# Attention stage of a four-stage kernel: from a barrier at each step to waits for producers, with a pair's work laid in five steps

## The chip, the cores and the metric

The program runs on one core of one Trainium2 chip. The time is device microseconds of one execution, from 3 runs of the kernel before. The core has four engines that compute, each with its own instruction queue that runs strictly in order: PE (TensorE), DVE (VectorE), ACT (ScalarE) and POOL (GpSimd); SP issues most transfers. Engines wait for one another by semaphores.

## The reference, cut to what matters

The model has four stages. Only the first, L0_attn, is touched. It takes x of 32 sequences x 256 tokens x 128 features:

```python
xn = _layernorm(x, ln1_g, ln1_b)
q = _l2norm((xn @ Wq).reshape(Bx, Tx, H, Dh))     # 16 heads of 8
k = _l2norm((xn @ Wk).reshape(Bx, Tx, H, Dh))
v = (xn @ Wv).reshape(Bx, Tx, H, Dh)
clock = softplus(xn @ clock_w + clock_b)
q, k = _rope(q, times), _rope(k, times)
gcp = exp(clip(cumsum(-softplus(xn @ gate_w + gate_b), axis=1), -60., 50.))
q, k = q * gcp, k / (gcp + 1e-08)
p = xn @ p_w + p_b
p_exp = exp(p - max(p, axis=1)) * clock
q = q / (cumsum(p_exp, axis=1) + 1e-08)
k = k * p_exp
attn = softmax(where(mask, einsum('bqhd,bkhd->bhqk', q, k) / sqrt(Dh), -inf))
x1 = einsum('bhqk,bkhd->bqhd', attn, v).reshape(Bx, Tx, D) @ out_w + out_b + x
h = _layernorm(x1, ln2_g, ln2_b)
return x1 + gelu(h @ mlp_w1 + mlp_b1) @ mlp_w2 + mlp_b2
```

The second stage norms each token, picks one of 8 experts by the largest affinity and applies it; the kernel computes affinity and place of a token at the end of attention and scatters its row there. Then come a state-space layer (the scan stage) and a coupling network with gelus.

## The kernel before

The function attention() works on pairs of sequences: 16 pairs (PAIRS) of 512 tokens (STEP), held as 4 tiles (TS) of 128 tokens, or turned, as 128 features x 512 tokens. Each engine runs a function of its own (pe_step, act_step, dve_step, pool_step, sp_step) once per step k, in an order written out by hand. In step k four things run side by side:

- the front of pair k: layer norm (bn statistics, a root as Ln and Exp on ACT, xn), the transposes into xt, projections for gate, clock, p, q, k, their swapped forms for the rotation, and v, each into bank FA or FB by turns; softplus as Abs, Exp, Ln; the running sums; q_t, the masked copies k_m (L723) and v_a (L711). POOL makes xl, the residual with the first norm, which goes to HBM and comes back as xlb_m.
- the scores of pair k-1: eight quads. quad(n) (L431) writes four scores blocks into the four RING banks, exps(n) (L606) takes them through Exp to es, weigh(n) (L450) multiplies them with v_a into the one bank AV. After two quads ACT copies AV out (av_copy), PE turns it back (back, L467), and DVE divides by the sums (heads_out, L733).
- the tail of pair k-2: o_tok turned, times out_w, x1, its norm h_tok, MLP (four times up, gelu, all through the one bank M, then down, L543), x2, its norm y_n, y1 (row), its norm xl2, the affinities (L586). mv_m, rs_m, stats_m, h_tok, o_t and M are single.
- the route of pair k-3: the best expert, its rank by a small matmul into AV (L488), the position, and four indirect DMAs from POOL (L921).

q_t, k_m, v_a, x_in, row and o_tok exist twice; xt, rot, mag, log, pre, factor, lnorm, square and pexp once. Gelu needs another table of ACT than Exp and Ln: a table is loaded at L664 and back at L665, and at the head of each step (L594).

At the end of a step each engine drains and raises end_pe, end_act, end_dve or end_pool, and begin() (L372) lets none start the next step before all four have. The steps are k = 0 to 18: four written out, a loop Fori with two steps in its body (k = 4 to 15), three written out. SP loads x_in one pair ahead, and xlb_m and x_m, once DVE and POOL have ended the step before.

## Time and profile before

| what | us |
|---|---|
| median of 3 runs (lowest, highest) | 2848.79 (2848.25, 2849.33) |
| the profiled execution's own time | 2853.14 |
| its span | 2851.4 |
| PE / DVE / ACT / POOL busy over the span | 2018.1 / 1834.8 / 1576.2 / 1162.6 |
| mean granted TensorE clock | 0.867 |

The page shows one profiled execution. Its slices of 71 us show the attention stage as the first fifteen: PE at 6 to 7 tenths, ACT at 5 to 6, DVE at 5. A timeline row gives start, duration, engine, line, operation, written and read tile and their shape; xN means that N instructions were merged; in brackets stands how long the engine idled ahead of it and what ended that. "<-issue" is a wait for nothing that the profile shows, "ACTq" the queue of an engine at its drain. The granted clock is 1.0 at 2.4 GHz and 0.5 at 1.2 GHz. L594 runs at the start of a step on ACT and so marks the steps: 42.6, 84.3, 134.2, 193.1 (k = 3), then every 60 to 62 us to 988.4 (k = 16), 1031.6 and 1068.3.

### The profile page before, as it was taken

Reading aid. Unit: us, or ns where it says so; the run is one execution under the profiler, and the core shown is the slowest. Engines: PE = TensorE matmul, PEld = TensorE weight load, DVE = VectorE, ACT = ScalarE, POOL = GpSimd, SP = SyncE. Lnnn points to the kernel's source line nnn. Section 1 sums busy time; section 2 is a strip of 40 time slices with the busy share of each in tenths; the row PEclk is TensorE's granted clock in tenths of the full one; section 3 lists DMA queues with packets and bytes.
Section 4 is the critical chain, followed back from the end, with each engine's and each line's share of the span. In section 5 each row is a group of like instructions: output and inputs, shape, how many; then the busy total and the mean of one; then the engine's idle time right before and its main releaser. Section 6 shows DMA issues by size and latency. Waiting matters only on the chain. (4 is left out here: it accounts for less than half of the span.)

```text
span 2851.4 us, 39979 instructions
## 1 busy us (share of the span) xinstructions
PE 2018.1 (71%) x11854; PEld 1037.9 (36%) x11909; DVE 1834.8 (64%) x3731; ACT 1576.2 (55%) x2903; POOL 1162.6 (41%) x718
## 2 busy tenths in 40 slices
PE   2677777777777763666646787777777777658886
PEld 0344444444444443556522222222222222124432
DVE  5565665555565522222225999999999999946665
ACT  1566666566666642444436666666666666435443
POOL 1111211211221112344325888888888878710000
PEclk7799998889899886888878899989999998878887
DMA  3000000000000001111111111112121111011111
GB/s 121 23 16 20 23 21 27 27 20 20 21 22 20 24 16 33 37 45 41 37 49 47 48 49 41 41 44 56 47 55 40 40 41 49 22 34 30 45 37 45
DMA packets 137060, 105.16 MB, mean 37 GB/s; under 512 B 12872, under 2 KB 130776, under 8 KB 136544
## 3 DMA queue, kind: packets, MB, share of 16 engines
q1 hardware_dynamic: 131424, 89.48, 11.3%
q0 software_dynamic: 5504, 13.90, 1.4%
q8 instruction: 85, 1.39, 0.2%
q14 instruction: 47, 0.39, 0.0%
HBM read 42.18 MB, written 27.59 MB: 24 GB/s over the span
## 5 line engine op out<-in xcount | busy, mean ns | idle before, releaser
L1738 POOL TENSOR_TENSOR hc<-h,c_rep 128x1024 f32<-128x1024 f32 x256 | 602.4, 2369 | 157.4 <-DVE h L1696 150.0
L1696 DVE TENSOR_TENSOR_SCAN h<-decay,bank 128x1024 f32<-128x1024 f32 x256 | 572.6, 2268 | 0.0
L1582 ACT ACTIVATE decay<-bank,neg_a_r 128x510 f32<-128x510 f32 x512 | 322.4, 682 | 323.4 <-PE bank L1473 275.8
L1687 DVE TENSOR_TENSOR bank<-bank,b_rep 128x1024 f32<-128x1024 f32 x256 | 304.3, 1216 | 53.7 <-PE bank L1460 53.0
L1460 PE MATMUL bank<-u,sel_u 128*128 128x512 bf16 x489 | 166.1, 421 | 234.9 <-DVE h L1696 227.9
L613 ACT ACTIVATE es<-bank 128x384 f32<-128x384 f32 x512 | 208.5, 493 | 52.9 <-PE bank L447 52.6
L1460 PEld LDWEIGHTS bank<-u,sel_u 128*128 128x128 bf16 x512 | 33.6, 99 | 408.5 <-DVE h L1696 363.7
L1473 PE MATMUL bank<-d,sel_u 128*128 128x512 bf16 x481 | 168.8, 424 | 6.4 <-ACT decay L1582 2.2
L901 POOL TENSOR_TENSOR xl<-x_in,f_mean_var 128x512 f32<-128x512 f32 x16 | 17.0, 1062 | 363.3 <-ACT f_rstd L604 363.3
L914 POOL TENSOR_TENSOR mag<-mag,one_up 128x512 f32<-128x512 f32 x16 | 20.5, 1282 | 338.7 <-ACT one_up L675 338.7
L1487 PE MATMUL bank<-hc,y_sel 128*32 128x512 f32 x1024 | 146.7, 647 | 4.6 <-POOL hc L1738 4.6
L424 PE MATMUL bank<-xt,w_a 128*128 128x512 f32 x224 | 135.8, 709 | 17.5 <-DVE pre L806 9.1
L1281 DVE SCALAR_TENSOR_TENSOR o<-bank,xs,xls 128x128 f32<-128x128 f32 x72 | 25.1, 349 | 177.6 <-PE bank L1148 89.2
L1234 ACT ACTIVATE hid<-bank 128x512 f32<-128x512 f32 x72 | 43.0, 597 | 169.0 <-PE bank L1136 165.7
L1494 PE MATMUL bank<-xpad,w_conv 128*128 128x512 f32 x256 | 124.4, 620 | 2.9 <-ACT xc L1625 1.4
L1124 PE MATMUL bank<-consts,xns 128*128 128x128 f32 x72 | 25.8, 360 | 138.6 <-ACT xns L1220 118.2
L439 PE MATMUL bank<-q_t,k_m 32*128 32x256 f32 x1024 | 103.3, 476 | 28.5 <-ACT es L613 23.1
L738 DVE RECIPROCAL rec<-bank 128x16 f32<-128x16 f32 x64 | 16.5, 257 | 157.7 <-PE bank L471 157.2
L1183 POOL COPY w_tile<-w 128x512 f32 x72 | 44.2, 614 | 177.1 <-PE bank L1136 160.5
L1903 PE MATMUL bank<-r_o_t,w_c 128*128 128x512 f32 x96 | 73.7, 885 | 41.4 <-DVEq L2114 20.6
L1136 PE MATMUL bank<-xst,w_tile 128*128 128x128 f32 x576 | 100.2, 329 | 0.0
L921 POOL DMA_INDIRECT rows_in_dram<-row,idx x64 | 76.6, 1197 | 52.2 <-DVEq L891 28.0
(333 smaller groups left out, 4727.4 us busy)
## 6 DMA issues: line engine op xcount, KB each, us to landing
xvs<-xv SPq DMA_DIRECT2D x16, 512.0 KB, 3.0
xs<-rows_in_dram SPq DMA_DIRECT2D x72, 68.0 KB
w<-in_w_dram SPq DMA_DIRECT2D x2, 2048.0 KB
x_in<-in_x_dram SPq DMA_DIRECT2D x16, 256.0 KB
xlb_dram<-xl SPq DMA_DIRECT2D x16, 256.0 KB, 2.3
xlb_m<-xlb_dram SPq DMA_DIRECT2D x16, 256.0 KB, 3.8
x_m<-in_x_dram SPq DMA_DIRECT2D x16, 256.0 KB, 3.7
g_xn<-yx_dram SPq DMA_DIRECT2D x16, 256.0 KB
```

The lines of the kernel that those rows point to most:

```text
L424: pe.matmul(bank[:, :], weight, xt[:, :], start=True, stop=True).then_inc(sem, 1)
L439: pe.matmul(RING[st][:, 0:T], kk[:, 0:P], q, start=True, stop=True, tile_position=(32 * st, 0))
L613: last = act.activation(es[(n % 2) * HS + st][:, :], RING[st][:, 0:3 * P], ACT.Exp, scale=DH ** -0.5)
L1136: last = pe.matmul(bank[:, f * P:(f + 1) * P], w1[j][:, f * P:(f + 1) * P], xt[j][:, :], start=False, stop=True, skip_group_check=True)
L1460: last = pe.matmul(BD[n % 2][:, i * STEP:(i + 1) * STEP], c["sel_u"][:, r, :], u3[p if n < NS else q][:, hf, st + i, :], start=True, stop= ...
L1473: pe.matmul(DL[i], c["sel_u"][:, r, :], d3[p if n < NS else q][:, hf, st + i, :], start=True, stop=True).then_inc(s["n_d"], 1)
L1487: last = pe.matmul(Y[32 * st:32 * st + 32, :], c["y_sel"][:, r, :], hc[(2 * i + st // 2) % 4][:, st % 2, :], start=False, stop=r == 3, til ...
L1494: last = pe.matmul(seq(G), c["w_conv"][:, tap, hf * P:(hf + 1) * P], xpad[:, :, tap:tap + T], start=tap == 0, stop=tap == TAPS - 1)
L1582: act.activation(decay[n % 4][:, i, :, 1:], seq(DL[i])[:, :, 1:], ACT.Exp, scale=c["neg_a_r"][:, hf, g:g + 1]).then_inc(s["n_da"], 1)
L1687: dve.tensor_tensor(pair_of(BD[n % 2]), pair_of(BD[n % 2]), b_rep[p if n < NS else q][:, :].unsqueeze(1).to_broadcast([P, 2, STEP]), ALU.m ...
L1696: dve.tensor_tensor_scan(flat(h[n % 4]), decay[n % 4].rearrange("p i b t -> p (i b t)"), BD[n % 2], 0.0, ALU.mult, ALU.add).then_inc(s["n_ ...
L1738: pool.tensor_tensor(hc[n % 4][:, :, :], h[n % 4][:, :, :], c_rep[p][:, :].unsqueeze(1).to_broadcast([P, 2, STEP]), ALU.mult).then_inc(s[" ...
```

## The change

begin(), the four end semaphores and the drains are gone. Every wait now names a producer, or by since(), which leaves out counts that are not positive, the last reader of a tile that is to be written again. The flags of a step are ln, front, scores, late, mid, tail, and a pair runs through five steps: its norm and xt in step k-1, its front in k, quads 0 to 5 and weighs 0 to 4 in k+1, the rest of the scores, heads_out(2) and (3) and x1 with its statistics in k+2 (late, mid), h_tok, MLP, y1, affinities and scatter in k+3 (tail). The steps are k = -1 to 18: six written out, a loop of four rounds with two steps (k = 5 to 12), six written out. There are a second xt and a tile rot_k beside rot; xn and o_tok are turned through M, the ranks go to FA instead of AV. SP loads x_in two pairs ahead. The table load at the head of a step is gone; Abs of mag stands ahead of the fourth gelu.

The written orders of a full step, with u the pair of the scores (k-1), w that of the late part (k-2):

- PE: gate; turn h_tok; clock; up(0); p; up(1); q; up(2); weigh(5,w); up(3); quad(6,w); down; back(2,w); quad(7,w); q swapped; weigh(6,w); weigh(7,w); quad(0,u); turn xn; ones for q; back(3,w); quad(1,u); k; weigh(0,u); turn xl2; weigh(1,u); quad(2,u); k swapped; back(0,u); quad(3,u); affinities; ones for k; weigh(2,u); weigh(3,u); turn o_tok; quad(4,u); ranks; out_w; back(1,u); quad(5,u); v; weigh(4,u).
- ACT: v_a; h_t; gelus 0 to 2; Abs; gelu 3; table; Exp and Ln of mag; exps(6,w); av_copy(2,w); pexp; square q; root ln; exps(7,w); one_up three times; exps(0,u); av_copy(3,w); root of x2; xt; exps(1,u); root of y1; lgcp twice; exps(2,u); av_copy(0,u); o_t; square k; Ln pcs; Ln lnorm; exps(3,u); neg; Exp factor q; o_t; exps(4,u); av_copy(1,u); Ln lnorm; exps(5,u); root of x1; Exp factor k; k_m.
- DVE: h_tok; pre twice; pmax, pneg; statistics of x_in; softplus and sum of the gate; heads_out(2,w); first of q's rotation; x2 and statistics; xn; y_n, y1, statistics; rest of q's rotation; heads_out(3,w); xl2; lnorm q; the clock's softplus, pexp, pcs; first of k's rotation; factor q; heads_out(0,u); affinities and best expert; rest of k's rotation; positions; q_t; lnorm k; factor k; x1 and statistics; heads_out(1,u); rot_k times factor, times pexp.
- POOL: xl in three; mag and log; four scatters; x1b.

The diff, cut to its core:

```diff
@@ attention @@
-        def begin(eng, k):
...
-            for sem in (s["end_pe"], s["end_act"], s["end_dve"], s["end_pool"]):
-                eng.wait_ge(sem, k)
+        def since(eng, sem, count):
...
+            if not isinstance(count, int) or count > 0:
+                eng.wait_ge(sem, count)
...
-        xt = sb("xt", [P, STEP])
+        xt = [sb(f"xt{n}", [P, STEP]) for n in range(2)]
...
+        rot_k = sb("rot_k", [P, STEP])
...
+        def pe_step(pe, k, half, p, ln, front, scores, late, mid, tail):
...
             if front:
+                pe.wait_ge(s["f_xt_sb"], k + 1)
+                since(pe, s["f_mk"], k)
+                project(FB, c["w_gate"], s["f_gate"])
             if tail:
+                pe.wait_ge(s["m_h"], k - 2)
+                transposes(M, h_tok, s["m_ht"])
+            if front:
+                since(pe, s["f_vaug"], k)
+                project(FA, c["w_clock"], s["f_clock"])
             if tail:
+                up(0)
...
+            if late:
+                weigh(5, k - 2, p)
+            if late:
+                quad(6, k - 2, p)
...
+            if late:
+                back(2, k - 2)
+                quad(7, k - 2, p)
+            if front:
+                pe.wait_ge(s["f_pe"], k + 1)
+                project(FB, c["w_qs"], s["f_qs"])
+            if late:
+                weigh(6, k - 2, p)
+            if late:
+                weigh(7, k - 2, p)
+                quad(0, k - 1, q)
+            if ln:
+                pe.wait_ge(s["f_xn"], k + 2)
+                if tail:
+                    pe.wait_ge(s["m_x2"], k - 2)
+                transposes(M, xn, s["f_xt"])
...
+            if late:
+                back(3, k - 2)
+                quad(1, k - 1, q)
+            if front:
+                pe.wait_ge(s["f_rb"], k + 1)
+            if scores:
+                weigh(0, k - 1, q)
...
+            if scores:
+                weigh(1, k - 1, q)
+                quad(2, k - 1, q)
+            if front:
+                pe.wait_ge(s["f_mq"], k + 1)
+                back(0, k - 1)
+                quad(3, k - 1, q)
...
+                weigh(2, k - 1, q)
+            if scores:
+                weigh(3, k - 1, q)
+            if mid:
+                pe.wait_ge(s["s_o"], 8 * k - 8)
+                if tail:
+                    pe.wait_ge(s["m_aff_sb"], k - 2)
+                elif ln:
+                    pe.wait_ge(s["f_xt_sb"], k + 2)
+                transposes(M, o_tok[p], s["m_ot"])
+            if scores:
+                quad(4, k - 1, q)
+            if tail:
+                pe.wait_ge(s["r_hot"], k - 2)
...
-            pe.drain().then_inc(s["end_pe"], 1)
...
+        def act_step(act, k, half, p, ln, front, scores, late, mid, tail):
...
+            if scores:
+                act.wait_ge(s["f_v"], k)
...
+                act.activation(v_a[q][:, :, :, 0:DH], FA.rearrange("p (j h d) -> p j h d", j=TS, h=H), ACT.Copy).then_inc(s["f_vaug"], 1)
+                act.wait_ge(s["m_ht"], k - 2)
...
+                act.activation(h_t[:, :], M[:, :], ACT.Identity, scale=c["ln2_g"], bias=c["ln2_b"]).then_inc(s["m_ht_sb"], 1)
...
+                for n in range(FC):
+                    if n == FC - 1 and front:
+                        act.wait_ge(s["f_pre1"], k + 1)
...
+                        act.activation(mag[:, :, :], pre[:, :, :], ACT.Abs).then_inc(s["f_abs"], 1)
+                    act.wait_ge(s["m_up"], 4 * k + (n - 11))
+                    act.activation(g[:, n, :], M[:, :], ACT.Gelu, bias=c["mlp_b1"][:, n:n + 1]).then_inc(s["m_gelu"], 1)
+                act.preload_act_table_set(EXP_LN)
...
+            if late:
+                exps(6, k - 2)
+                av_copy(2, k - 2)
...
+            if late:
+                exps(7, k - 2)
...
+            if scores:
+                exps(0, k - 1)
+            if late:
+                av_copy(3, k - 2)
+                root(mv_m[:, :, 1], ln_m[:, :], rs_m[:, :], s["m_mv2"], s["m_ln2"], s["m_rs2"], k - 2, bias=EPS)
...
+                exps(1, k - 1)
+            if tail:
+                root(vv_m[:, :, :], vv_m[:, :, :], row[q][:, :, RS0:RS1 + 1].rearrange("p j v -> p v j"), s["m_vv3"], s["m_ln3"], s["m_rs3"], k - 2)
...
+                exps(2, k - 1)
+                av_copy(0, k - 1)
...
+                exps(3, k - 1)
+            if tail:
+                act.wait_ge(s["r_neg"], k - 2)
+                act.activation(neg[:, :], neg[:, :], ACT.Exp).then_inc(s["r_exp"], 1)
...
+                exps(4, k - 1)
+                av_copy(1, k - 1)
+            if front:
+                act.wait_ge(s["f_mk"], k + 1)
+                exps(5, k - 1)
+            if mid:
+                root(mv_m[:, :, 1], ln_m[:, :], rs_m[:, :], s["m_mv"], s["m_ln"], s["m_rs"], k - 1, bias=EPS)
...
+                act.wait_ge(s["f_zk"], k + 1)
+                act.wait_ge(s["f_k2"], k + 1)
...
+                    last = act.activation(k_m[p][:, v, :], rot_k[:, :], ACT.Copy, scale=c["head_mask"][:, v:v + 1])
...
+        def dve_step(dve, k, half, p, ln, front, scores, late, mid, tail):
...
+            if late:
+                heads_out(2, k - 2, p)
+            if front:
+                turned(rot, FA, FB, s["f_ra"], s["f_sq"], s["f_rb"], s["f_qs"], s["f_rq"], 0)
...
+                dve.wait_ge(s["m_dn"], k - 2)
+                dve.tensor_tensor(x2[:, :, :], tok(M), x1b[:, :, :], ALU.add).then_inc(s["m_x2"], 1)
...
+            if ln:
+                dve.wait_ge(s["f_rs"], k + 2)
...
+                centred(xn, x_in[q], mv, rs[:, 1, :], s["f_xn"])
+            if tail:
+                dve.wait_ge(s["m_rs2"], k - 2)
+                centred(h_tok, x2, mv_m, rs_m, s["m_yn"])
...
+                dve.tensor_tensor(row[q][:, :, 0:D], h_tok[:, :, :], x_m[:, :, :], ALU.add).then_inc(s["m_y1"], 1)
...
+                stats_of(dve, row[q][:, :, 0:D], stats_m, mv_m, s["m_st3"], s["m_mv3"], k - 2)
+                two_variances(dve, vv_m, mv_m[:, :, 1], s["m_vv3"])
+            if front:
+                turned(rot, FA, FB, s["f_ra"], s["f_sq"], s["f_rb"], s["f_qs"], s["f_rq"], 1)
+            if late:
+                heads_out(3, k - 2, p)
...
+                                         row[q][:, :, RS0:RS1 + 1], ALU.mult, ALU.mult)
+                centred(xl2, row[q][:, :, 0:D], mv_m, row[q][:, :, RS0], s["m_xl2"])
...
+            if scores:
+                heads_out(0, k - 1, q)
+            if tail:
+                dve.wait_ge(s["m_aff"], k - 2)
+                dve.tensor_copy(aff[:, :, :], M[:, 0:TS * E].rearrange("p (j e) -> p j e", j=TS)).then_inc(s["m_aff_sb"], 1)
...
+                turned(rot_k, FB, FA, s["f_ka"], s["f_sk"], s["f_kb"], s["f_ks"], s["f_rk"], 1)
+                chain(dve.tensor_tensor(pos[:, :, :], FA[:, 0:TS * E].rearrange("p (j e) -> p j e", e=E),
...
+                dve.tensor_tensor(q_t[p][:, :], rot[:, :], factor[:, :], ALU.mult).then_inc(s["f_qt"], 1)
...
+                dve.tensor_scalar(lnorm[:, :], FB[:, :], 1e-24, None, ALU.max).then_inc(s["f_mk"], 1)
...
+                dve.scalar_tensor_tensor(factor[:, :], lnorm[:, :], -0.5, lgcp[:, :], ALU.mult, ALU.subtract).then_inc(s["f_zk"], 1)
...
+                dve.wait_ge(s["m_ow"], k - 1)
...
+                dve.tensor_tensor(x1[:, :, :], tok(M), xlb_m[:, :, :], ALU.add).then_inc(s["m_x1"], 1)
...
+                stats_of(dve, x1, stats_m, mv_m, s["m_st"], s["m_mv"], k - 1)
+                heads_out(1, k - 1, q)
...
+                dve.tensor_tensor(rot_k[:, :], rot_k[:, :], factor[:, :], ALU.mult).then_inc(s["f_k1"], 1)
...
+                dve.tensor_tensor(rot_k[:, :], rot_k[:, :], pexp[:, :], ALU.mult).then_inc(s["f_k2"], 1)
...
+            def one(k, half, p):
+                step(eng, k, half, p, k < PAIRS - 1, 0 <= k < PAIRS, 1 <= k < PAIRS + 1, 2 <= k < PAIRS + 2, 2 <= k < PAIRS + 2, 3 <= k)
...
+            for k in range(-1, 5):
+                one(k, k // 2, k % 2)
+            with eng.Fori(0, (PAIRS - 8) // 2) as n:
+                step(eng, n * 2 + 5, n + 2, 1, True, True, True, True, True, True)
+                step(eng, n * 2 + 6, n + 3, 0, True, True, True, True, True, True)
+            for k in range(PAIRS - 3, PAIRS + 3):
+                one(k, k // 2, k % 2)
```

## Rows read from the trace of the kernel before

**Rows 1.** The table of windows: both stretches, then busy us (x instructions) per engine.

```profile
core 0: us, PE busy (x) PEld busy (x) DVE busy (x) ACT busy (x) POOL busy (x), PEclk, DMA share, GB/s
193.10:988.40 795.30, 604.81 (x5292) 367.61 (x5293) 463.70 (x1470) 503.21 (x1015) 159.01 (x130) 0.90 0.08 23
1000.00:1032.00 32.00, 25.82 (x287) 16.49 (x284) 8.21 (x41) 18.31 (x40) 2.87 (x3) 0.97 0.03 10
```

**Rows 2.** Timeline of PE: start us, us, instruction; the first matmul of two steps.

```profile
621.76 1.09 PE L428 MATMUL bank<-consts,o_tok 128*128 128x128 f32 x4 [4.10 <-issue]
...
681.75 0.66 PE L428 MATMUL bank<-consts,o_tok 128*128 128x128 f32 x2 [1.84 <-ACTq L725]
```

**Rows 3.** Timeline of PE, then ACT, where only scores ran.

```profile
1013.42 0.71 PE L439 MATMUL bank<-q_t,k_m 32*128 32x256 f32 x8
...
1014.83 0.64 PE L459 MATMUL bank<-es,v_a 128*32 128x256 f32 x8
...
1015.29 0.40 PE L463 MATMUL bank<-es,v_a 128*32 128x128 f32 x8
...
1014.61 1.64 ACT L613 ACTIVATE es<-bank 128x384 f32<-128x384 f32 x4 [2.00 <-PE bank L447]
...
1018.99 0.63 ACT L620 ACTIVATE avs<-bank 128x512 f32<-128x512 f32 x1
```

**Rows 4.** Timeline of ACT in one full step.

```profile
632.67 0.21 ACT L602 ACTIVATE m_ln<-m_mean_var 128x4 f32<-128x4 f32 x1 [3.05 <-DVE m_mean_var L387]
...
638.14 1.06 ACT L648 ACTIVATE mag<-mag 128x1024 f32<-128x1024 f32 x1
...
644.95 0.69 ACT L664 ACTIVATE g<-bank,vec 128x512 f32<-128x512 f32 x1 [1.22 <-PE bank L479]
...
649.47 1.28 ACT L665 ACT_TABLE_LOAD   x1
...
679.06 2.55 ACT L723 ACTIVATE k_m<-rot,consts 128x512 f32<-128x512 f32 x4
```

**Rows 5.** Timeline of PE in the same step.

```profile
637.37 0.60 PE L428 MATMUL bank<-consts,h_tok 128*128 128x128 f32 x4
...
644.75 1.02 PE L424 MATMUL bank<-xt,w_a 128*128 128x512 f32 x2
645.69 1.12 PE L479 MATMUL bank<-h_t,w_a 128*128 128x512 f32 x2
```

**Rows 6.** Timeline of DVE, then POOL, in the same step.

```profile
623.86 3.79 DVE L755 TENSOR_SCALAR xn<-x_in,f_mean_var,f_rstd 128x128 f32<-128x128 f32 x4 [1.63 <-ACT f_rstd L604]
630.62 0.69 DVE L784 TENSOR_TENSOR x<-bank,xlb_m 128x512 f32<-128x512 f32 x1 [2.98 <-PE bank L501]
...
634.25 0.18 DVE L793 TENSOR_TENSOR pos<-bank,fill 128x32 f32<-128x32 f32 x1
...
635.63 0.72 DVE L806 TENSOR_SCALAR pre<-bank,vec 128x512 f32<-128x512 f32 x1
...
660.70 1.11 DVE L755 TENSOR_SCALAR h_tok<-x,m_mean_var,m_rstd 128x128 f32<-128x128 f32 x4
...
664.20 0.26 DVE L738 RECIPROCAL rec<-bank 128x16 f32<-128x16 f32 x1
...
623.99 1.11 POOL L901 TENSOR_TENSOR xl<-x_in,f_mean_var 128x512 f32<-128x512 f32 x1 [23.17 <-ACT f_rstd L604]
```

**Rows 7.** Timeline of PE: the same work in two neighbouring steps.

```profile
605.74 2.03 PE L565 MATMUL bank<-square,consts 128*128 128x512 f32 x2 [2.05 <-DVE rot L747]
...
668.41 1.12 PE L565 MATMUL bank<-square,consts 128*128 128x512 f32 x2 [2.05 <-DVE rot L747]
```

**Rows 8.** Timelines of ACT, DVE and POOL at the stage's two ends.

```profile
84.31 1.28 ACT L594 ACT_TABLE_LOAD   x1
...
1038.60 1.11 DVE L755 TENSOR_SCALAR h_tok<-x,m_mean_var,m_rstd 128x128 f32<-128x128 f32 x4 [0.58 <-ACT m_rstd L604]
...
1078.45 0.96 POOL L921 DMA_INDIRECT rows_in_dram<-row,idx  x1 [0.30 <-issue]
```

More of the change, by code:

```diff
@@ L566, in pe_step @@
-            if scores:
-                quad(6)
-                weigh(5)
-            if front:
-                pe.wait_ge(s["f_kb"], rf)
-                for j in range(TS):
-                    last = pe.matmul(FA[:, j * P:(j + 1) * P], xt[:, j * P:(j + 1) * P], c["w_v"], start=True, stop=True)
-                last.then_inc(s["f_v"], 1)
-            if scores:
-                back(2)
-                quad(7)
-                weigh(6)
-            if tail:
-                pe.wait_ge(s["m_xl2"], rm)
-                transposes(M, xl2, s["m_x2t"])
@@ new lines, in pe_step @@
+            if mid:
+                pe.wait_ge(s["m_ot_sb"], k - 1)
+                for j in range(TS):
+                    last = pe.matmul(M[:, j * P:(j + 1) * P], o_t[:, j * P:(j + 1) * P], c["w_o"], start=True, stop=True)
+                last.then_inc(s["m_ow"], 1)
+            if scores:
+                back(1, k - 1)
+                quad(5, k - 1, q)
+            if front:
+                pe.wait_ge(s["f_kb"], k + 1)
+                if tail:
+                    pe.wait_ge(s["r_pos"], k - 2)
+                for j in range(TS):
+                    last = pe.matmul(FA[:, j * P:(j + 1) * P], xt[p][:, j * P:(j + 1) * P], c["w_v"], start=True, stop=True)
+                last.then_inc(s["f_v"], 1)
@@ new lines, in act_step @@
+            if front:
+                if not tail:
+                    act.wait_ge(s["f_pre1"], k + 1)
+                    since(act, s["f_soft"], k)
+                    act.activation(mag[:, :, :], pre[:, :, :], ACT.Abs).then_inc(s["f_abs"], 1)
+                act.wait_ge(s["f_abs"], k + 1)
+                act.activation(mag[:, :, :], mag[:, :, :], ACT.Exp, scale=-1.0).then_inc(s["f_exp"], 1)
+                act.wait_ge(s["f_exp"], k + 1)
+                since(act, s["f_sp"], k)
+                act.activation(log[:, 0, :], mag[:, 0, :], ACT.Ln, bias=1.0).then_inc(s["f_log"], 1)
```

598 lines of the change are left out of this document (245 added, 353 removed).

## The prediction

> **What bounds the kernel now.** I read the page's slices first: the attention stage ends near 1080 us [rows 8], and nothing behind it is touched. Then the table of windows over its thirteen full steps (k = 3 to 15): 795.3 us, 61.2 each, in which TensorE (PE) is busy 46.5, ScalarE (ACT) 38.7, VectorE (DVE) 35.7 and GpSimd (POOL) 12.2 [rows 1]. No engine is full; even PE lacks 24%. So the handing over between engines sets the step, the barrier being one part of it. What the barrier alone costs is seen on PE: it idles 1.84 us ahead of a step's first matmul, and 4.10 where the loop jumps back [rows 2]. That is some 3 us of a step's 14.7 us of PE idleness; the other 12 lie inside the step, where PE waits for ACT's exponentials and copies and for DVE's rotations and norms. Taking the barrier away is worth 3 us at most; the rest depends on whether the new order shortens the way work goes round the engines.
>
> **What sets the new step.** Without a barrier a step's length is the longest closed round of waits: from one instruction to the same one a step later, along each engine's written order and each semaphore. I walked the new order from the listing with the durations of the old one. The prices:
> - a quad takes PE 1.41 us until the next operation (1013.42 to 1014.83), and lets its exponentials start after 1.19; a weigh takes 0.86 (1014.83 to 1015.69); four exponentials 1.62, a copy of AV 0.62 [rows 3];
> - a root 0.45, a table load 1.28, an exponential of 128x1024 1.07, one gelu 0.69, the four k_m copies 2.6, one 128x512 activation 0.6 to 0.65 [rows 4];
> - four transposes 0.53 to 0.6, a projection 0.94 (644.75 to 645.69), an up-projection 1.12, 1.16 until its gelu can start [rows 5];
> - a DVE pass over 128x512 0.7, x1 with its statistics 2.05 (630.62 to 632.67), y_n to the two variances 3.5 (660.70 to 664.20), xl2 1.2, the position chain 1.4 (634.25 to 635.63), one heads_out 0.6 [rows 4, 6].
>
> The longest round that I find closes over 16 legs, from weigh(3) to weigh(3):
> 1. PE: weigh(3), transposes of o_tok, quad(4), ranks: 0.86 + 0.53 + 1.41 + 0.4 = 3.2
> 2. DVE: positions, q_t, lnorm for k: 1.4 + 0.7 + 0.7 = 2.8
> 3. ACT: Ln of lnorm: 0.65
> 4. DVE: factor for k, then x1 and statistics: 0.7 + 2.05 = 2.75
> 5. ACT: root, Exp of factor: 1.1
> 6. DVE: two products into rot_k: 1.4
> 7. ACT: k_m, then v_a: 2.6 + 0.6 = 3.2
> 8. PE: clock projection, into the bank that v_a frees, up(0): 0.94 + 1.16 = 2.1
> 9. gelu and up in turn on the one bank M, each with a projection or weigh(5) between: 2.1 + 2.1 + 2.0 + 0.7 = 6.9
> 10. ACT: table load, Exp and Ln of mag, exps(6), AV copy: 1.28 + 1.07 + 0.55 + 1.6 + 0.6 = 5.1
> 11. PE: back(2), quad(7), q's swapped projection, weigh(6), weigh(7), quad(0): 0.55 + 1.41 + 0.94 + 1.72 + 1.19 = 5.8
> 12. ACT: exps(0), AV copy, root for y_n: 2.7
> 13. DVE: the y_n block, second half of q's rotation, heads_out(3), xl2: 3.5 + 1.4 + 0.6 + 1.2 = 6.7
> 14. PE: transposes, weigh(1), quad(2): 2.6
> 15. ACT: exps(2), AV copy: 2.25
> 16. PE: back(0), quad(3), affinities, ones product, weigh(2) behind heads_out(0): 0.55 + 1.41 + 1.0 + 1.0 + 0.86 + 0.3 = 5.1
>
> The legs sum to 54.4, and some ten hand-overs of 0.05, seen from a gelu's end at 645.64 to PE's start at 645.69 [rows 4, 5], make 55.0. So the order still goes round the engines in series; it is shorter than the old one, not free.
>
> **The clock.** These are prices at TensorE's 2.4 GHz. The granted clock of the full steps was 0.90, so a fifth of the time lay at the 1.2 GHz level; at that level the same product took 2.03 us instead of 1.12 [rows 1, 7]. PE's legs above hold about 25 us, so a share f at the lower level adds 25 x 0.8 x f. Where PE was busy 81% of a stretch the grant was 0.97, f = 0.06 [rows 1]; the new steps would be busy some 44 of 56, 79%. I take f = 0.08: 1.5 us, and a step of 56.5.
>
> **What else moves.** The second xt and the second rotation tile let work start early; they add no instruction. The x_in load is issued two pairs ahead and xlb_m and x_m behind the readers of their tiles; each has tens of us to land, so SP's queue costs nothing, and if a load were late it would stand before DVE's x1 or y1, on the round. POOL's four instructions of scatter keep their length; x1b now stands behind them and is needed only at x2, over 25 us later. The table load at each step's start goes, but it ran while ACT had to wait for PE's first transposes anyway, so nothing is gained. Abs now stands between two gelus. No row shows an Abs under the gelu table; if it forces two loads, they cost 2.56 a step on leg 9, if not zero. I take zero. The Trainium skill (ScalarE: Activation LUTs, Table sets) says that cheap functions such as abs are in every set; no row here shows it. POOL's arithmetic slows DVE: xn took 3.79 for four instructions beside xl, y_n of the same shape 1.11 without [rows 6]. xn runs now in a gap in which DVE would wait for leg 12's root, at no cost; x1b may fall on leg 6 or on h_tok, 0 to 2.5 us, and I take 0. The loop jumps back 3 times instead of 5; PE's jump cost 2.3 us, and PE has some 2.5 us of slack at that place of the new round, so I count 0, between -5 (two jumps fewer) and +7 (three in full) in all.
>
> **Both ends.** Before, step 0 ended at 84.3, and the full steps began at 193.1 [rows 1, 8]. Step 0 must still go once through a pair's front; the norm of pair 1 now lies in it and its 3.79 of xn delays q's rotation: it ends near 87. Step 1 has its norm behind it and only six quads, by the same walk 36; step 2 adds quads 6 and 7 with their copies and x1: 45. So the thirteen full steps begin at 168. Behind them, step 16 is the round without the front's legs 2 to 8 in part, 11 and 13 in part: 42. Step 17 is a lone MLP, in the old trace 32 us from its h_tok at 1038.60 to the end of its affinities, and 5 for the next pair's x1: 37. Step 18 is h_tok to the last scatter, 1038.60 to 1079.4: 41 [rows 8]. A last pair that is spread over more steps thus gives back some 28 us of what the full steps gain.
>
> **The sum.** 168 + 13 x 56.5 + 42 + 37 + 41 = 1022.5, where the last scatter ended at 1079.4 [rows 8]: 56.9 us saved. The profiled execution took 2853.1 (span 2851.4), 4.3 over the median of 2848.8; so 2796.2 in a profile, 2791.9 as a median, say 2792.
>
> **The rivals.**
> - PE becomes the bound, 0.16. If a leg of my round isn't on it (an engine that comes early and lets two legs overlap), the step falls towards PE's own 44 to 46.5. At 47 the end is at 168 + 611 + 120 = 899, 180 earlier: 2668; at 52, between, 2733. For it: PE's 46.5 is all that is unavoidable. Against: ACT, DVE and PE take turns in the round, in written order.
> - The clock stays as it was, 0.14. With f = 0.20 PE's legs rise by 25 x 0.8 x 0.2 = 4.0: 59.0 a step, 2824. For it: drops follow waits of 2 us as short as that ahead of L565, which once ran slow and once fast [rows 7].
> - Slower than before, 0.09. Place: PE's legs. Instead of a long idle stretch at each barrier PE now has many of 1 to 2 us, and if these keep it at 1.2 GHz for half the time, a step costs 55 + 10 = 65, and the total is 2848.8 + 13 x 65 + 288 - 1079.4 = 2902. It decides from 60.9 a step (791.4 / 13), f = 0.30. Against: 0.97 at 81% busy. The Trainium skill (TensorE: Matmul & The Clock Gate, A second HAM failure mode) tells of a kernel whose short idles between matmul groups made the clock swing; by that rule this rival, by the row at 1000 us the forecast.
> - The change doesn't do what it says: a wait for the slowest engine survives, each step near 60.5, within 0.2% of before, 0.03.
>
> **How the numbers follow.** The forecast, 54 to 58.5 a step (2759 to 2818), has 0.58. The range reaches into the faster case to 52.3 a step and into the clock's to 59.5: 2737 to 2830; outside stay most of PE's case and the slower one, some 0.2. A difference of 0.2% (5.7 us) is about what a measurement of this kernel can tell from none. Faster: 0.58 + 0.16 + 0.14 = 0.88; within: 0.03; slower: 0.09.
>
> **What would show it.** Right: full steps of 54 to 58 us; PE idle ahead of the clock projection for v_a, ahead of k's projection for rot_b, and ahead of weigh(2) and weigh(4) for DVE; a granted clock of 0.94 or more in the full steps; the last three steps about 120 us together. Wrong: a step of 50 or less with PE over 90% busy (a leg isn't on the round); a granted clock of 0.90 or less; table loads beside Abs; or a stage end that comes over 130 us after the last k_m.

## The result, and the profile after

The changed kernel took 2828.84 us (median of 4, 2823.87 to 2829.27) beside 2849.06 for the kernel before: a ratio of 0.9918, with a 95% interval from 0.9899 to 0.9937. So 20 us are saved; the prediction had 57. In the two profiled executions it is 24.4 (2853.14 and 2828.72; spans 2851.4 and 2826.9).

All times below come from three marks in each trace: the end of ScalarE's k_m copies of pair 2 (start of the thirteen full steps), the same of pair 15 (their end), and the end of the last scatter (the end of the stage). For the kernel before the marks are those of [rows 1, 8]. Behind the last scatter the span has 1772.8 us after and 1772.0 before: nothing changed there.

| us | before | forecast | after |
|---|---|---|---|
| start | 193.1 | 168 | 172.0 |
| 13 full steps (one) | 795.3 (61.2) | 734.5 (56.5) | 744.2 (57.24) |
| the rest, to the last scatter | 91.0 | 120 | 137.9 |
| stage | 1079.4 | 1022.5 | 1054.1 |

The windows of the changed kernel: the full steps, and then the three steps in which the last pairs run out (us, then busy us and instructions of each engine, the granted clock, DMA share, GB/s).

```profile
core 0: us, PE busy (x) PEld busy (x) DVE busy (x) ACT busy (x) POOL busy (x), PEclk, DMA share, GB/s
172.00:916.00 744.00, 590.11 (x5285) 362.66 (x5285) 482.24 (x1453) 483.09 (x998) 145.19 (x127) 0.90 0.08 23
916.00:972.00 56.00, 39.95 (x376) 24.75 (x377) 15.88 (x73) 24.00 (x54) 5.14 (x5) 0.77 0.05 15
972.00:1013.00 41.00, 25.66 (x170) 15.68 (x169) 13.00 (x67) 12.99 (x26) 3.54 (x4) 0.67 0.04 12
1013.00:1054.00 41.00, 18.57 (x61) 11.10 (x59) 8.94 (x47) 7.73 (x13) 5.40 (x6) 0.54 0.02 7
```

The clock of the full steps is what it was in [rows 1], 0.90. DVE is busy 482 us in them where it had 464 in 51 us more: its instructions became longer (it is 462 once x1b is moved, see below). The last three rows are nearly steps 16, 17 and 18. The clock falls to 0.54 in them, near its 1.2 GHz level throughout.

Where leg 6 of the round lies, DVE and POOL (timelines; start, duration):

```profile
677.73 2.28 DVE L972 TENSOR_TENSOR rot_k<-rot_k,factor 128x512 f32<-128x512 f32 x1 [0.26 <-ACT factor L782]
680.04 0.69 DVE L974 TENSOR_TENSOR rot_k<-rot_k,pexp 128x512 f32<-128x512 f32 x1
...
677.18 0.96 POOL L998 DMA_INDIRECT rows_in_dram<-row,idx  x1 [0.30 <-issue]
678.17 1.28 POOL L1003 TENSOR_TENSOR x1b<-x,rows 128x512 f32<-128x512 f32 x1
```

The first of two products of one shape takes 2.28 us, the second 0.69. The first lies beside POOL's x1b, which runs right behind the scatters until 679.45. It is on the round: k_m waits for it. At the end of step 16 x1b lies beside h_tok instead, which takes 2.84 us there and 1.11 elsewhere (DVE, then POOL):

```profile
968.45 2.84 DVE L819 TENSOR_SCALAR h_tok<-x,m_mean_var,m_rstd 128x128 f32<-128x128 f32 x4 [2.29 <-issue]
...
969.15 1.27 POOL L1003 TENSOR_TENSOR x1b<-x,rows 128x512 f32<-128x512 f32 x1
```

k_m and the jump of the loop:

```profile
623.39 2.56 ACT L786 ACTIVATE k_m<-rot_k,consts 128x512 f32<-128x512 f32 x4 [3.14 <-DVE rot_k L974]
...
620.60 0.43 PE L478 MATMUL bank<-es,v_a 128*32 128x128 f32 x8
624.46 2.07 PE L435 MATMUL bank<-xt,w_a 128*128 128x512 f32 x2 [3.43 <-issue]
...
677.62 1.08 PE L474 MATMUL bank<-es,v_a 128*32 128x256 f32 x8 [2.14 <-DVE o_tok L805]
```

These are ScalarE, then TensorE, at a jump of the loop. PE stands 3.43 us for nothing that the profile shows, where in [rows 2] it was 4.10; then the clock projection runs at 1.2 GHz (2.07; 0.94 to 1.02 in [rows 5]). The last row is the wait for DVE ahead of weigh(4) that the prediction named.

Gelu's table load stands in two ways. First a pass of the loop, then a step that is written out (ScalarE):

```profile
628.30 1.28 ACT L678 ACT_TABLE_LOAD   x1
630.38 0.69 ACT L678 ACTIVATE g<-bank,vec 128x512 f32<-128x512 f32 x1 [0.80 <-PE bank L494]
...
634.78 1.05 ACT L676 ACTIVATE mag<-pre 128x1024 f32<-128x1024 f32 x1
636.10 0.69 ACT L678 ACTIVATE g<-bank,vec 128x512 f32<-128x512 f32 x1 [0.27 <-PE bank L494]
...
744.64 1.28 ACT L678 ACT_TABLE_LOAD   x1 [3.25 <-PE bank L494]
745.94 0.69 ACT L678 ACTIVATE g<-bank,vec 128x512 f32<-128x512 f32 x1
```

In the loop the load runs while up(0) runs. In the written-out steps from k = 4 on it stands behind the wait for up(0), and the whole 1.28 us come on top. What decides the place isn't shown: step 3, written out, waits only for up(0) and has the load early (173.15); step 4 waits for w_down's reader too and has it late (233.26); but the steps of the loop have both waits in the program and the load early. Abs (L676) stands between two gelus, and no load comes with it.

### The profile page after: what moved, and what is told of

The parts are those of the page before. It is cut to its first block and busy times, and to the rows that moved or that the text cites. A ratio compares the mean times of both kernels' runs of the same rounds, so it can differ in the third digit from the quotient of the medians.

```text
span 2826.9 us, 39859 instructions
## 1 busy us (share of the span) xinstructions
PE 2013.0 (71%) x11854; PEld 1035.8 (37%) x11909; DVE 1861.9 (66%) x3731; ACT 1552.1 (55%) x2885; POOL 1154.5 (41%) x718
## 5 line engine op out<-in xcount | busy, mean ns | idle before, releaser
L998 POOL DMA_INDIRECT rows_in_dram<-row,idx x64 | 66.5, 1039 | 434.7 <-DVE row L947 420.0
L435 PE MATMUL bank<-xt,w_a 128*128 128x512 f32 x224 | 152.5, 777 | 39.9 <-ACT v_a L666 20.4
L474 PE MATMUL bank<-es,v_a 128*32 128x256 f32 x1024 | 85.6, 405 | 39.2 <-DVE o_tok L805 35.8
L494 PE MATMUL bank<-h_t,w_a 128*128 128x512 f32 x128 | 90.9, 799 | 15.9 <-ACT g L678 12.6
L1224 PE MATMUL bank<-w,hid 128*128 x576 | 95.4, 317 | 1.1 <-ACT hid L1310 1.1
```

The lines of the kernel that those rows point to most:

```text
L435: pe.matmul(bank[:, :], weight, xt[p][:, :], start=True, stop=True).then_inc(sem, 1)
```

## The experiments

Each kernel is one or more edits of the changed kernel and computes the same. They ran in four groups, each beside the kernel before on its own chip (there 2838.8 to 2840.8), so the totals are compared as ratios and the stages by their marks. The changed kernel itself was run again beside the second group.

| kernel | ratio to before [95%] | start | one full step | rest | stage |
|---|---|---|---|---|---|
| the change | 0.9918 [0.9899, 0.9937] | 172.0 | 57.24 | 137.9 | 1054.1 |
| after_same_chip | 0.9905 [0.9889, 0.9922] | 171.2 | 57.24 | 134.4 | 1049.7 |
| barrier_back | 0.9998 [0.9987, 1.0009] | 175.6 | 58.39 | 148.0 | 1082.6 |
| x1b_later | 0.9792 [0.9773, 0.9810] | 171.4 | 54.89 | 134.1 | 1019.0 |
| xl_later | 0.9883 [0.9864, 0.9902] | 165.6 | 57.01 | 133.7 | 1040.4 |
| gelu_table | 0.9874 [0.9858, 0.9891] | 172.3 | 56.52 | 130.9 | 1038.0 |
| root_early | 0.9904 [0.9887, 0.9920] | 172.3 | 57.12 | 133.2 | 1048.2 |
| all | 0.9763 [0.9747, 0.9779] | 165.9 | 54.55 | 122.4 | 997.5 |
| warm | 0.9863 [0.9846, 0.9879] | 170.7 | 56.83 | 125.6 | 1035.1 |
| unrolled | 0.9952 [0.9934, 0.9971] | 170.7 | 58.02 | 134.4 | 1059.4 |
| gelu_unrolled | 0.9864 [0.9843, 0.9886] | 172.1 | 56.51 | 131.5 | 1038.3 |
| warm_unrolled | 0.9849 [0.9826, 0.9872] | 171.4 | 56.29 | 125.5 | 1028.7 |
| all_unrolled | 0.9749 [0.9730, 0.9767] | 165.3 | 54.60 | 128.6 | 1003.8 |
| all_warm | 0.9741 [0.9717, 0.9765] | 167.5 | 55.04 | 115.7 | 998.7 |
| all_warm_unrolled | 0.9638 [0.9614, 0.9663] | 167.4 | 52.75 | 118.9 | 972.0 |
| all_barrier | 0.9832 [0.9810, 0.9853] | 169.0 | 54.91 | 143.8 | 1026.7 |

> The changed kernel itself, beside its variants. Both theories expect what was measured before: a ratio to the kernel before of 0.990 to 0.994, an attention stage of about 1054 us to the end of the last scatter, full steps of 57.2 us each. If this chip gives a stage under 1045, the gains read so far (x1b_later 36 us, gelu_table 17, xl_later 14.6) hold a part that is the chip's, and what has to be taken off them is the difference.

The stage came out 4.4 us shorter, 3.5 of it in the rest; the full steps agree to 0.1 us in 744. So full steps compare across chips, the rest to 3 or 4 us only.

### The barrier

```
+ for sem in (end_pe, end_act, end_dve, end_pool): eng.wait_ge(sem, k + 1)   # ahead of each step
  inner(eng, k, ...)
+ eng.drain().then_inc(end_<engine>, 1)
```

> The changed kernel with a drain and a barrier over the four engines at every step, as in the kernel before; the five-step order stays. Theory (the gain comes from the overlap across the step's boundary: gate and h_tok run beside k_m): the chain gate, h_tok, its transposes, h_t then starts behind k_m, 3 to 5 us more per step over 20 steps, total 2890 to 2930, slower than the kernel before. Rival (the order gives the gain and the barrier costs only what was seen before it, 1 to 3 us a step): 2850 to 2880.

Measured: 0.9998. With the barrier, the new order is no faster than the kernel before, as far as this can tell. In a full step the barrier costs 1.15 us only (58.39 against 57.24), below the theory's 3 to 5 and at the low end of the rival's 1 to 3; the total lies just below the rival's 2850 (0.9998 of 2849). The barrier costs 4 us more at the start and 10 to 14 in the rest. The profiled execution lay 6.7 us above the median of barrier_back, so the marks make the barrier dear rather than cheap.

### x1b beside rot_k

```
- if mid: x1b = x1 + row          # POOL, behind the scatters
+ if tail: wait h_tok(k - 2); x1b = x1 + row      # first in the next step
```

> x1b moves on POOL from behind the scatter to the head of the next step, behind h_tok. In the trace of the changed kernel DVE's product rot_k times factor takes 2.28 us beside x1b (678.17 to 679.45), the next one 0.69. Theory (contention on the longest round): the product falls to 0.69 in the 13 full steps with x1b beside it, k_m starts 1.6 us earlier, the full steps fall from 57.2 to 55.6 and the total by about 20 us, to 2809 from 2829. Rival 1 (the product isn't on the round that sets the step): it falls to 0.69, the step stays at 57.2, total unchanged. Rival 2 (x1b only collides elsewhere): another DVE instruction at the head of the step grows by about 1.3 us and the total stays.

```profile
663.80 0.69 DVE L972 TENSOR_TENSOR rot_k<-rot_k,factor 128x512 f32<-128x512 f32 x1 [0.26 <-ACT factor L782]
664.52 0.69 DVE L974 TENSOR_TENSOR rot_k<-rot_k,pexp 128x512 f32<-128x512 f32 x1
...
666.33 1.27 POOL L982 TENSOR_TENSOR x1b<-x,rows 128x512 f32<-128x512 f32 x1 [2.13 <-DVE h_tok L819]
...
171.36:884.92 713.56, 566.62 (x5285) 356.19 (x5285) 462.33 (x1453) 482.65 (x1000) 144.86 (x127) 0.94 0.08 24
```

DVE, POOL and the window of the full steps. The product is at 0.69 again, the step 2.35 us shorter, 30.6 over thirteen: the 1.59 of the instruction and some more, with the clock up to 0.94. That is more than the theory's 1.6. This one collision is larger than what the barrier gives in the full steps.

### xn beside xl

```
- POOL: xl; mag, log(front); scatters          + POOL: mag, log(front); [wait pcs] xl; scatters
```

> POOL's three instructions for xl move behind mag and log and wait for pcs, where DVE waits for ACT. In the changed kernel the four xn instructions take 4.18 us beside xl. My prediction said that this costs nothing, since DVE would wait for the root of x2 anyway. Theory A (prediction): xn falls to about 1.1 us, DVE then waits for the root, the steps stay within 0.3 us of 57.2, total unchanged within 5 us. Theory B (xn delays PE's transposes by 2.4 us, with that quad(1), exps(1) and the root behind it, on which xl2 waits 1.4 us): the full steps fall by 1.4 to 2.4 us, the total by 18 to 30 us.

The instructions of xn fall from a mean of 1101 ns to 342. The group of them in ten steps of the changed kernel (busy us, mean ns, idle before):

```profile
L819 DVE TENSOR_SCALAR xn<-x_in,f_mean_var,f_rstd 128x128 f32<-128x128 f32 x40 | 41.7, 1101 | 0.4
```

and the same group in xl_later:

```profile
L819 DVE TENSOR_SCALAR xn<-x_in,f_mean_var,f_rstd 128x128 f32<-128x128 f32 x40 | 11.2, 342 | 0.4
```

DVE has 3 us less to do in a step, and the step is 0.2 shorter. It waits instead for the root ahead of y_n, as the prediction said. That is not all of it. Three rows of the changed kernel and of xl_later (TensorE and VectorE in the first, TensorE in the second):

```profile
650.01 0.94 PE L439 MATMUL bank<-consts,xn 128*128 128x128 f32 x4 [2.36 <-DVE xn L819]
...
656.80 0.17 DVE L894 SCALAR_TENSOR_TENSOR row<-m_mean_var,row 128x8 f32<-128x8 f32 x1 [1.37 <-ACT row L646]
...
704.33 1.43 PE L435 MATMUL bank<-xt,w_a 128*128 128x512 f32 x2 [2.49 <-DVE rot_b L813]
```

In the changed kernel TensorE waits 2.36 us for xn; quad(1), exps(1) and the root of y1 behind it come late, and xl2 waits 1.37 for that root. So leg 13 takes 8.1 us, where xl_later has 6.6. But xl_later gives most of it back in leg 14 (3.7 for 2.6): TensorE now waits 2.49 ahead of k's projection, and this projection, weigh(0) and the transposes of xl2 run slow. Theory B had the chain right and missed what stood behind it.

The start gains 6 us (steps 1 and 2 are 3.8 and 1.5 us shorter); I read this as xn having no other work to hide behind there.

### The table load

```
  h_t = ...                                     # ACT
+ load the gelu table here
  wait up(0); gelu
```

> The table for gelu is asked for explicitly behind h_t, ahead of the waits for down and up. In the changed kernel's trace the table load stands behind the wait for up(0) in seven written-out steps (k = 4 and 13 to 18) and beside up(0) in the others. Theory (it lies on the longest round): 7 x 1.25 = 9 us less, total 2820. Rival (slack elsewhere takes it up): the load moves ahead in the seven steps, and the total stays within 2 us of 2829.

0.72 us a full step and 3 to 7 in the rest. In the loop the load was hidden already: the gain lies in the written-out steps, where the changed kernel's steps 4, 13, 14 and 15 took 58.4, 58.4, 58.4 and 59.1 and these take 56.9, 55.8, 57.0 and 56.8. unrolled is the cross-check: the same instructions with the loop's four passes written out as eight steps.

```
- with eng.Fori(0, (PAIRS - 8) // 2) as n: step(n * 2 + 5); step(n * 2 + 6)
+ for k in range(5, PAIRS - 3): step(k)
```

> The changed kernel with its loop of 4 passes written out as 8 steps; the same instructions in the same order. At the top of each pass TensorE stands still for 3.4 us with no wait that the profile shows. Theory (this is the jump, and it is hidden: the clock projection behind it starts 1.5 us ahead of k_m's end, and VectorE's rot_k closes the round): the 3.4 us turn into waits for VectorE, a full step stays between 56.9 and 57.4, the stage at 1046 to 1051 on a chip that gives 1050. Rival (the jump also costs the later engines and lets the clock fall): the four passes give back 1.5 to 3.4 us each, full steps 56.2 to 56.8, the stage 1037 to 1044.

Neither side had it: 58.02, more than with the loop. Its ScalarE shows why.

```profile
576.61 0.76 ACT L670 ACTIVATE h_t<-bank,vec 128x512 f32<-128x512 f32 x1
580.28 1.28 ACT L678 ACT_TABLE_LOAD   x1 [2.91 <-PE bank L494]
581.58 0.69 ACT L678 ACTIVATE g<-bank,vec 128x512 f32<-128x512 f32 x1
```

Written out, every step has the late load.

> gelu_table with the loop written out. unrolled took 58.0 us a step where the kernel with its loop took 57.2, and the first gelu's table load stands behind the wait for up(0) in it (580.28 to 581.56, the gelu at 581.58). Theory (written out, each of the 8 steps pays the late load, 1.3 to 1.6 us, and saves the jump's 0.5 or so): with the load ahead of the wait full steps take 56.2 to 56.7, at least 1.3 us less than unrolled's. Rival (writing the loop out costs by itself, in instructions fetched): 57.2 or more, no more than 0.8 less than unrolled's.

With the load ahead of the wait 58.02 becomes 56.51, which is gelu_table's 56.52 with the loop. So the load is worth 1.5 us where it is late, and without it the loop as such costs nothing.

### The root ahead of exps(5)

root_early puts x1's root ahead of exps(5) in steps 16 and later.

> In the steps without a front (16 and later) the root of x1's variance is put ahead of exps(5) on ScalarE; nothing else is changed. Theory (in step 16 h_tok, and behind it the transposes of xl2, wait for this root, which stands behind exps(5) for 2.5 us): the end shrinks by 2 to 4 us, from 138 to 134 to 136, full steps unchanged at 57.2, the stage 1050 to 1052. Rival (the end is set by TensorE's slow clock, not by this root): the stage stays at 1053 to 1055.

1.2 us in the rest, below what repeats of one kernel differ by: it can't be told from nothing. The theory's 2 to 4 us are not borne out.

### The clock

```
+ def fill(bank, src, times): times x matmul(bank, w_gate, src)     # written over before it is read
  # 2 ahead of the gate projection, 2 of xn's transposes, 1 of xl2's, 2 of weigh(4);
  # steps without a front: 1 ahead of up(1), 1 of up(2)
```

> Eight matmuls of 512 columns with no use are put into TensorE's waits of each full step (2 before the gate projection, 2 before the transposes of xn, 1 before those of xl2, 2 before weigh(4), 1 or 2 between the ups in the steps without a front); nothing else is changed. Theory (the 1.2 GHz stretches come of TensorE's waits, and the round pays them in its TensorE legs): the granted clock of the full steps rises from 0.90 to 0.95 or more, legs 1, 8, 11 and 16 shrink by some 2 to 3 us together, a full step goes from 57.2 to 54.5 to 56, the end from 138 to 130, the stage from 1054 to 1010 to 1035. Rival (the waits are waits for VectorE, and what fills them only stands in front of the next matmul): the clock rises or not, but a full step stays at 57 to 59 and the stage at 1050 to 1075.

A full step holds seven of these matmuls, not eight as written there. The granted clock rose to 0.98, and the rest fell by 9 us, from 134.4 to 125.6. The full steps split in two kinds. The windows of warm, a step without a jump and the next one, behind a jump:

```profile
455.08:509.84 54.76, 44.02 (x411) 27.15 (x411) 36.89 (x112) 37.18 (x78) 11.48 (x10) 0.99 0.09 26
509.84:571.20 61.36, 53.01 (x431) 30.90 (x431) 38.31 (x114) 37.30 (x79) 11.49 (x10) 0.95 0.08 23
```

54.8 is 2.4 below the average of the changed kernel; 61.4 gives it back. PE's row at the jump:

```profile
627.42 3.78 PE L444 MATMUL bank<-xt,w_a 128*128 128x512 f32 x4 [6.37 <-issue]
```

The jump took 3.43 us behind a wait of 2 us for DVE; with that wait filled it takes 6.37 and then runs at 1.2 GHz (four passes of 128x512 in 3.78; 1.88 at full speed).

> warm with the loop written out. In warm the steps behind a jump took 61.3 to 61.6 us, those with none in front 54.8. Theory (the filled waits take away the time in which TensorE's queue gets over the jump, 6.4 us of standing still in the place of 3.4, and the clock's gain is all there in the other steps): every full step takes 54.8 to 55.5, 13 of them 712 to 722, the stage 1010 to 1020, a ratio of 0.976 to 0.981. Rival (the 61.4 is an even and odd pattern of the buffers, not the jump): the pattern of 54.8 and 61.4 stays, full steps 56.8, the stage 1035.

The steps of 61 are gone, the longest is 57.6: it was the jump. The average is 56.29 and not 55; the late load is back in each step and may be the difference.

### All four, with and without the clock and the loop

> x1b_later, xl_later, gelu_table and root_early in one kernel. Theory (four costs in different places of the round, each with the legs it took alone): 1054.1 - 36 - 14.6 - 17 - 3 = 983 at the least; since part of each single gain was the clock, which can't rise above 1.0, I expect 990 to 1010 for the stage, full steps of 53 to 54.5, a ratio of 0.970 to 0.976. Rival (x1b's collision and the late table load hide each other's gain, since both let the round close earlier only as far as TensorE's own work allows, which was 45.4 us of busy time in a step of 57.2): full steps stay at x1b_later's 54.9 and the stage at 1010 to 1020, a ratio of 0.977 to 0.981.

54.55 a step, 122.4 for the rest, 997.5. Beside after_same_chip the stage is 52 us shorter, the sum of the four single gains 53. By parts they don't add: a full step gains 2.7 of 3.4, the rest 12 where the single ones gave 6 (in all_unrolled, below, it gains 6 too).

> all, with warm's matmuls in it, the loop kept. Theory (the jump is exposed where TensorE has no slack): steps without a jump at 52.5 to 53.5, those behind a jump at 57 to 60, full steps 54.3 to 55.5 on average, no gain over all's 54.55; the end shorter by the clock, 114 to 118 in the place of 122; the stage 985 to 998. Rival (TensorE bound: 8 more matmuls on 45 us of busy time cost their own 3.4 us each step): full steps of 57 to 58 everywhere, the stage above 1015.

Steps without a jump 53.2, those behind one 61.0 to 62.3 (the theory had 57 to 60), in the mean 55.04; the rest 115.7.

> all, with warm's matmuls, the loop written out. Theory (with the jump gone the warm clock's 2 us and the four repairs add up): full steps of 52.0 to 53.5, 13 of them 676 to 696, the end 114 to 118, the stage 955 to 980, a ratio of 0.962 to 0.970. Rival (TensorE's own work bounds: 45 to 48 us busy plus its short waits): full steps stay at 54 to 55, the stage at 985 to 997, a ratio of 0.972 to 0.976.

52.75 a step and 972.0 for the stage, as the theory had it; the rest, 118.9, lies 1 us over.

> all with its loop written out, without the added matmuls. all took 54.55 us a step (53.7 without a jump, 55.6 behind one), all_warm_unrolled 52.75. Theory (jump and clock are two costs of about 1 us each, and add): full steps of 53.5 to 54.2, the stage 984 to 992, the granted clock 0.93 to 0.95. Rival (the slow stretches are there for the jump alone, and what the matmuls did is to move them): 52.6 to 53.2, as all_warm_unrolled.

The window of all_unrolled's full steps, and TensorE ahead of k's projection:

```profile
165.34:875.16 709.82, 591.11 (x5285) 356.15 (x5285) 424.65 (x1453) 482.38 (x1000) 143.88 (x127) 0.91 0.08 24
...
575.11 2.08 PE L435 MATMUL bank<-xt,w_a 128*128 128x512 f32 x2 [2.32 <-DVE rot_b L816]
```

The same two of all_warm_unrolled:

```profile
167.37:853.18 685.81, 606.47 (x5457) 371.72 (x5457) 425.02 (x1454) 482.31 (x999) 144.06 (x127) 1.00 0.08 25
...
563.10 1.13 PE L435 MATMUL bank<-xt,w_a 128*128 128x512 f32 x2 [1.42 <-DVE rot_b L831]
```

The clock goes from 0.91 to 1.00 and the step from 54.60 to 52.75, although TensorE got more work. That is what the clock gives back, less what the added matmuls cost themselves: 1.85 us a step. Without the four edits the same pair of kernels, unrolled and warm_unrolled, gives 1.73 (58.02 to 56.29, clock 0.91 to 0.98). all_unrolled met neither side: all's 54.55 with the loop and 54.60 without are the same, so the jump, exposed as it is there (53.7 without one, 55.6 behind one), costs nothing in the mean. The granted clock is 0.93 with the loop and 0.91 without, so I take it that the gap at the jump and the slow clock elsewhere trade places. all_warm_unrolled is the fastest kernel of this study: 2739.42 us (2733.49 to 2742.09) beside 2840.78.

> all_unrolled with the four engines' end and begin semaphores of the kernel before put back at every step. In the changed kernel they cost 1.2 us in a full step. Theory (they cost little since every engine's last work in a step is close to the round's closing leg, and the x1b collision no more hides them): 1.5 to 3.0 us a step over all_unrolled, the stage 1020 to 1040. Rival (the barrier is hidden by the round, whatever else is repaired): 0.5 to 1.3 us a step, the stage 1000 to 1015. Third (the one that the prediction had: the order only pays without the barrier, which with shorter legs stops more engines): 3.5 to 4.5 us a step, the stage above 1045.

Beside all_unrolled the barrier costs 0.31 us in a full step, 3.7 at the start and 15.2 in the rest. Two rows of TensorE in all_barrier, the first product behind the border and k's projection of the same step, and one of all_unrolled, its clock projection:

```profile
387.86 2.05 PE L441 MATMUL bank<-xt,w_a 128*128 128x512 f32 x2 [3.49 <-ACTq L1023]
...
416.43 1.12 PE L441 MATMUL bank<-xt,w_a 128*128 128x512 f32 x2 [2.32 <-DVE rot_b L822]
...
602.60 2.07 PE L435 MATMUL bank<-xt,w_a 128*128 128x512 f32 x2 [0.93 <-ACT v_a L666]
```

At the border TensorE waits 3.49 us for ScalarE's drain behind k_m, and only then come the gate projection and h_tok's transposes. Without the barrier both run beside k_m (from 598.64 on), and the clock projection waits 0.93 for v_a. From the end of k_m to the first gelu it is 5.15 us with the barrier and 4.13 without: the border itself costs 1.0 us. The rest of the step gives it back (49.5 against 50.5 to the next end of k_m): k's projection, behind a wait of 2.3 us in both, takes 1.12 in twelve of thirteen steps of all_barrier and 2.08 in all thirteen of all_unrolled. The granted clock is 0.93 with the barrier and 0.91 without. So 0.31 is what is left of 1.0 us after the clock.

In the rest and at the start fewer pairs are under way to lie beside the barrier; that this is why it costs more there was not tried. The three parts make 22.9 us of the stage. The full steps fell below even the rival's 0.5, the stage into the range of the first theory, but by the rest and not by the steps.

## Why the prediction was right and wrong

**Right: direction, round, Abs.** "No engine is full" held (TensorE 79% of the full steps), and the trace waits in the order of the sixteen legs, but for leg 13. The step from the end of rot_k at 623.28 to that at 680.73 took 57.5 us against 56.4 forecast (54.4 + 0.5 + 1.5). The legs that differ by over 0.6 are leg 6 (3.0 for 1.4, x1b), leg 8 (3.9 for 2.1, at the jump and with TensorE at its lower clock) and leg 13 (8.1 for 6.7). Leg 13 left the path that was forecast: xl2 waited for the root of y1, which stood behind xn's transposes, quad(1) and exps(1), as shown at xl_later. Freed of the four costs and at full clock the step measured 52.75 where the legs have 55.0, so they had been priced some 2 us too long. That the full steps came out within 0.7 us of the forecast is therefore in part luck: costs that were left out met legs that were too long. Of the places where TensorE should wait, that ahead of k's projection shows in 4 of the 13 steps only. Abs under gelu's table cost nothing, as the prediction took it and the Trainium skill's page (ScalarE: Activation LUTs, Table sets) has it.

**Wrong: x1b taken at 0 (leg 6).** The prediction bounded it by "0 to 2.5 us, and I take 0". It was on the round and worth 2.35 us a step, 30.6 us in all; with x1b moved a step took 54.89, below the 56.5 that was forecast, so x1b alone doesn't explain the miss: the stage of 1019.0 is near the 1022.5 only because short steps met a long rest. The reason given, that x1b "is needed only at x2, over 25 us later", spoke of who waits for it, not of what it slows. [rows 6] had the pattern at xn, and POOL's scatters, whose length stays, put x1b beside leg 6 step after step. The Trainium skill (SBUF — State Buffer, Who interferes with whom) says that a DVE instruction with two inputs in SBUF contends with a GpSimd one that reads SBUF, and the loser waits for the whole instruction. The trace agrees in that the product, with both inputs in SBUF, took 2.28 and ended 0.56 behind x1b. The profile has the product start 0.44 us ahead of x1b, so which of the two came first can't be read from it. The other place that the prediction named, h_tok, was hit too, once: 2.84 us at the end of step 16.

**Wrong: the ends.** 168 + 120 became 172 + 137.9, the larger part of the miss. The three last steps, cut where the prediction cut them (end of k_m, start of h_tok twice, last scatter):

| us | step 16 | step 17 | step 18 |
|---|---|---|---|
| forecast | 42 | 37 | 41 |
| the change | 52.3 | 42.9 | 42.7 |
| after_same_chip | 51.4 | 40.2 | 42.8 |
| gelu_table | 50.5 | 39.5 | 40.9 |
| warm | 50.5 | 37.7 | 37.3 |
| all | 46.2 | 35.6 | 40.7 |
| all_unrolled | 49.9 | 38.4 | 40.4 |
| all_warm | 42.7 | 35.6 | 37.4 |

The step that failed most is step 16, the one that was walked by legs at 2.4 GHz: 10.3 us over, with a clock of 0.77. Steps 17 and 18 had been read from the old trace, its slow stretches included (clock 0.59 from 1038.60 to 1079.4), and came nearer. Step 18 misses by the late table load; step 17 in part by it and by the h_tok of 2.84 us, which the repeat doesn't have. In step 16 the early load and the filled waits took off 0.9 us each; the four edits and the filled waits together bring it to 42.7, so nearly all of the 10 us can be had back in this order. How they divide stays open: all and all_unrolled differ by 3.7 us in this step. Over the whole rest the filled waits took off 8.8 us, the early load 3 to 7, the root nothing that can be told. At the start, xn beside xl is worth 6 us: "no cost" held in the full steps (0.2 us) and not there.

**Wrong: the clock.** f = 0.08, "a granted clock of 0.94 or more"; it stayed at 0.90, f = 0.20. The rival of an unchanged clock had put 4.0 us a step on it; filling the waits gave 1.73 and 1.85 back, the added matmuls' own cost taken off. 25 x 0.8 x f counts every slow matmul on TensorE's legs as on the round, but part of the slow ones stood in waits: the gate projection at 598.64 of all_unrolled took 1.91, and TensorE still waited 0.93 for v_a before the clock projection. So the error in f and the error in its price nearly cancelled, by luck: 1.5 forecast, some 1.8 measured. The slower rival, with f = 0.5 and 10 us, fell. What it rested on holds in kind: TensorE's short waits do cost clock, 1.85 us a step. The Trainium skill (TensorE: Matmul & The Clock Gate, A second HAM failure mode) tells of a kernel in which short idles between groups of matmuls made the clock swing. The traces agree: with the waits filled the clock rose from 0.91 to 1.00.

**Not in the sum: gelu's load.** Without the barrier gelu also waits for w_down's reader, and in the written-out steps that have this wait the load stands behind the wait for up(0): 1.5 us in each such full step, 0.7 in the mean of the thirteen. That the second wait moved it is not shown.

**Right, for the wrong reason: barrier and jump.** "3 us at most" held, with 1.15 in this kernel and 0.31 when the collisions are gone; but the bound from PE's idle time at the border said nothing on the work that moves behind the border, nor on the clock that gives part of it back. The jump's 0 held too, until the waits beside it are filled: then TensorE stands 6.4 us, and a step behind the jump is 6.6 us longer than one without in warm, 8 to 9 in all_warm.

**The sum.** 4 from the start, 9.7 from the full steps and 18 from the rest make the 31.6 us by which the stage ended later than forecast. All of the 24 that did come is what the barrier takes, since the order with the barrier put back gives 0.9998: its shorter full steps (2.8 us each, 36) and its shorter start (17) pay for its longer rest (57) and no more. Once the four costs are gone the order pays with the barrier too (all_barrier, 0.9832).

## What to carry to other kernels

When an order changes, write down for every GpSimd instruction which VectorE instructions lie beside it, not only who waits for it: one add that nobody waited for cost more in full steps than a barrier of four engines. Price the steps in which the pipeline runs out by the clock that sparse work gets, and ask of a barrier which work moves behind it and which of it would wait there anyway. When several small costs lie on one round, take them away together as well as singly: here each gave at most 31 us of the stage of 1049.7, and together with the clock and the written-out loop 78.

## What the runs showed of the hardware

- A VectorE product of 128x512 with both inputs in SBUF took 2.28 us beside a GpSimd add of 1.28, and 0.69 alone, though the profile has it start 0.44 us ahead of the add; xn, four normalisations of 128x128, 1101 ns each beside xl and 342 alone.
- A ScalarE table load that the program leaves implicit stood behind the instruction's pending wait in some steps and ahead of it in others: 1.5 us a step (58.02 to 56.51 with the load asked for ahead of the wait).
- Seven matmuls of no use in a step of 54.6 us made the step 1.85 us shorter, with the granted clock up from 0.91 to 1.00.
- TensorE stood 3.4 us at a loop's jump behind a wait of 2 us, and 6.4 us with that wait filled.
- With a barrier of four engines ahead of each step one projection later in the step ran in 1.12 us instead of 2.08, behind the same wait of 2.3 us, and gave back most of the 1.0 us that the border cost.
